# Cross attention over 16 batches on one core: the Gram matrix summed in the same PSUM banks, its turned part made by VectorE

## The chip, the core and the metric

The kernel runs on one core of a Trainium2 chip. The metric is the device time of one execution in microseconds, the median of three runs. In fp32r, TensorE's fast form of fp32, an operand is used with fewer bits than fp32 has; the kernel splits each operand into a hi and a lo part and adds two or three products.

## The reference

Sixteen batches, each with x and a context of 512 channels by 1024 columns. Cut to what is computed:

```python
g_x     = conv1x1(g_w, g_b, ctx).T          # (N, 256)
theta_x = conv1x1(theta_w, theta_b, x).T    # (N, 256)
phi_x   = conv1x1(phi_w, phi_b, ctx)        # (256, N)
W  = theta_x @ phi_x / N                    # (N, N)
y  = (W @ g_x).T                            # (256, N)
wy = conv1x1(w_w, w_b, y)                   # (512, N)
out = bn_gamma * (wy - bn_mean) / sqrt(bn_var + eps) + bn_beta + x
```

Since nothing but products stands between phi and g, the kernel never forms the N x N matrix. It forms the Gram matrix G = ctx ctx^T (512 x 512, symmetric), multiplies the small weights into it, and applies the 256 x 512 result to theta.

## The kernel before, in words

Each batch goes through these steps on TensorE, in this order in one queue.

1. **S and M.** The context lies turned in eight chunks of 128 columns, ctxT_hi and ctxT_lo. With H and L for the two parts, G = H^T H + H^T L + (H^T L)^T, the last product being left out. S = H^T H is formed only in the ten 128x128 blocks of HELD (s_chunk, 32 matmuls), in gbank0 to gbank2. M = H^T L is formed whole, four rows of 128x512, eight matmuls each, in M_BANK, which is wbank4 and wbank0 in turn.
2. **Column sums** of the context (two matmuls).
3. **Turned blocks.** ScalarE has copied M's rows to mt (m_rows); ten matmuls with an identity (`turned`) add the transposed blocks of M to S in the gbanks. VectorE then adds the plain blocks of M from mt and puts the ten finished blocks in stage (`gram_sum`, L534).
4. **First half of theta** (m = 0, its k = 0 and 1). Then six transposes by TensorE (L871) read stage and make the blocks of LOWER, the mirrored ones. They wait for gram_f32. Then the second half of theta, k = 2 and 3.
5. **T blocks** (`t_block`, four blocks of twelve matmuls) multiply G by the phi weights. They wait for gram_lo (L542, all three parts) and low_lo (L591), the lo parts of G that VectorE makes. The fourth T block waits for t_taken, VectorE's copy of the first T block out of its bank (L630).
6. The rest of theta, Q, and the output in eight parts, which VectorE adds to x (L689).

Beside this, for the next batch: VectorE turns the context chunks in 32x32 blocks (L504), ScalarE makes ctxT_hi (`next_hi`, at fixed places of its queue), GpSimd makes ctxT_lo and the running sum per chunk, and after them x_lo (L332). All orders are written out by hand, per engine; semaphores alone tie the engines together. The first batch has its own order (with FIRST_M_BANK) and is not touched by the change. L699 and L357 are the lines of the helpers for every matmul and every ScalarE copy.

Of the kernel before, what the change touches and what calls it, by code (L numbers as in the profile page):

```python
# [27 lines left out]
def xattn_kernel(nc, x, ctx_in, theta_w, theta_b, phi_w, phi_b, g_w, g_b, w_w, w_b,  # L28
# [26 lines left out]

    PLAIN = [(0, 3, 0), (3, 6, 5), (6, 9, 10), (9, 10, 15)]
    T_BANK = [0, 1, 2, 0]
    Q_BANK = [1, 2]
# [8 lines left out]
    with ExitStack() as ctx:  # L67
# [3 lines left out]
        def sem(name):  # L71
            return ctx.enter_context(nc.semaphore(name))
# [44 lines left out]
        scale = sb("scale", [P, KC])  # L117


        m_flat = mt[:, :, :].rearrange("p a b -> p (a b)")  # L120
        t_hi = mt[:, 0:2, :].rearrange("p a (b c) -> p (a b) c", b=2)
        t_lo = mt[:, 2:4, :].rearrange("p a (b c) -> p (a b) c", b=2)
# [34 lines left out]

        M_BANK = [wbank[4], wbank[0], wbank[4], wbank[0]]

# [40 lines left out]
        gram_row = sem("gram_row")  # L200
        m_done, m_made = sem("m_done"), sem("m_made")
        gram_f32 = sem("gram_f32")
        gram_hi_made, gram_lo_made = sem("gram_hi_made"), sem("gram_lo_made")
# [6 lines left out]
        out_done = sem("out_done")  # L210

        def f(ap):

            return ap.bitcast(F32)

# [7 lines left out]
        def gram_bank(place):  # L223

            i = min(place // 3, 2)
            at = place * P - BANK_SPAN[i][0]
            return gbank[i][:, at:at + P]

        def first(b):
# [125 lines left out]
        def _(act):  # L355
# [67 lines left out]
            def body(b, half, par, nxt, nxt2):  # L423
# [4 lines left out]

                def m_rows():
                    for i in range(KC):  # L430
                        if i < KC - 1:
                            act.wait_ge(m_done, (KC - 1) * b + (i + 1))
                        else:
                            next_hi(0)
                            act.wait_ge(gram_chunk, CH * b + CH)
                        hi(mt[:, i, :], M_BANK[i][:, :], m_made)

                def gram_hi_parts():
                    for i, (a, z) in enumerate(BANK_SPAN):
                        act.wait_ge(gram_f32, 3 * b + (i + 1))  # L440
                        hi(gram_hi[:, a:z], stage[:, a:z], gram_hi_made)

                if not first(b):
                    m_rows()
                    next_hi(1)
                    gram_hi_parts()
                    next_hi(2)
# [40 lines left out]
        def _(dve):  # L488
# [39 lines left out]
            def gram_sum(b, i):  # L528
# [7 lines left out]
                if i != 2:  # L536
                    ins.then_inc(gram_f32, 1)

            def gram_lo_part(b, i):
# [36 lines left out]
            def body(b, half, par, nxt, nxt2):  # L576
# [120 lines left out]
        def _(pe):  # L697
# [63 lines left out]
            def body(b, half, par, nxt, nxt2):  # L761
# [11 lines left out]
                if first(b):  # L773
                    for c in range(CH):
                        s_chunk(c)
                        if c == RING:
                            turn_vectors()
                        pe.wait_ge(first_lo, c + 1)
                        for i in range(KC):
                            ins = mm(FIRST_M_BANK[i][:, :], hi_of(c, i), ctxT_lo[:, c, :], c == 0, c == CH - 1)  # L780
                            if i == KC - 1:
                                ins.then_inc(gram_chunk, 1)
                            elif c == CH - 1:
                                ins.then_inc(m_done, 1)
                else:
                    pe.wait_ge(work_free, NO * b + (4 - NO))
                    for c in range(CH):
                        s_chunk(c)
                    for i in range(KC):
                        if i < 2:  # L790
                            pe.wait_ge(work_free, NO * b + ((5, 6)[i] - NO))
                        else:
                            pe.wait_ge(m_made, KC * b + (i - 1))
                        for c in range(CH):
                            if i == 0:
                                pe.wait_ge(ctxT_lo_made, CH * b + (c + 1 - CH))
                            ins = mm(M_BANK[i][:, :], hi_of(c, i), ctxT_lo[:, c, :], c == 0, c == CH - 1)
                            if i == KC - 1:
                                ins.then_inc(gram_chunk, 1)
                        if i < KC - 1:  # L800
                            ins.then_inc(m_done, 1)

# [164 lines left out]
```

## Time and profile before

| | us |
|---|---|
| median of three runs | 783.51 (783.49 to 783.71) |
| the profiled execution | 783.43 |
| its span, first to last instruction | 781.6 |
| TensorE busy | 773.8 (99%) |
| VectorE busy | 495.3 (63%) |
| ScalarE busy | 304.3 (39%) |
| GpSimd busy | 526.5 (67%) |

TensorE's matmuls overlap: a 128x512 one stands for 0.39 us in the rows, but the next starts 0.23 us behind it. So the time of a group of matmuls is read from start to start of the groups, not as a sum of durations. The same holds in a smaller way for VectorE.

### The profile page before, as it was taken

Reading aid. Unit: us, or ns where it says so; the run is one execution under the profiler, and the core shown is the slowest. Engines: PE = TensorE matmul, PEld = TensorE weight load, DVE = VectorE, ACT = ScalarE, POOL = GpSimd, SP = SyncE. Lnnn points to the kernel's source line nnn. Section 1 sums busy time; section 2 is a strip of 40 time slices with the busy share of each in tenths; the row PEclk is TensorE's granted clock in tenths of the full one; section 3 lists DMA queues with packets and bytes.
Section 4 is the critical chain, followed back from the end, with each engine's and each line's share of the span. In section 5 each row is a group of like instructions: output and inputs, shape, how many; then the busy total and the mean of one; then the engine's idle time right before and its main releaser. Section 6 shows DMA issues by size and latency. Waiting matters only on the chain.

```text
span 781.6 us, 11639 instructions
## 1 busy us (share of the span) xinstructions
PE 773.8 (99%) x4066; PEld 668.8 (86%) x4066; DVE 495.3 (63%) x891; ACT 304.3 (39%) x514; POOL 526.5 (67%) x358
## 2 busy tenths in 40 slices
PE   7999999999999999999999999999999999999998
PEld 6688888888888888888888888888888888888887
DVE  3874865749657385664848657396574847658255
ACT  5534533414344243543425345143542325334231
POOL 5939995757858477785758857478685767847500
DMA  9815573370835508264280734608365181740202
GB/s 278 202 67 130 194 188 135 79 245 1 215 107 110 212 22 216 84 161 161 54 252 17 188 134 90 232 0 215 107 132 190 33 229 59 173 150 1 108 1 107
DMA packets 55415, 103.17 MB, mean 132 GB/s; under 512 B 2506, under 2 KB 38244, under 8 KB 55396
## 3 DMA queue, kind: packets, MB, share of 16 engines
q1 hardware_dynamic: 53264, 101.86, 44.6%
q10 hardware_dynamic: 2132, 1.05, 0.6%
q8 instruction: 12, 0.20, 0.1%
q14 instruction: 7, 0.06, 0.0%
HBM read 69.35 MB, written 33.55 MB: 132 GB/s over the span
## 4 chain that ended last, share of the span: by engine, by line
PE 98%; DMA 1%; POOL 0%; DVE 0%; ACTq 0%; ACT 0%; issue 0%
PE wbank L699 58%; PE gbank L699 38%; PE wbank L871 1%; PE wbank L745 1%; DMA ctx_sb<-in_ctx_dram 1%; PE wbank L723 0%; PE wbank L751 0%; POOL ctxT_lo L303 0%; PE wbank L735 0%; DVE ctxT L504 0%; ACT ctxT_hi L357 0%; ACTq L368 0%; DVE x_sb L676 0%; ACTq L142 0%; PE wbank L710 0%
## 5 line engine op out<-in xcount | busy, mean ns | idle before, releaser
L303 POOL TENSOR_TENSOR ctxT_lo<-ctxT,ctxT_hi 128x512 fp32r<-128x512 f32 x124 | 168.0, 1356 | 202.9 <-ACT ctxT_hi L357 202.9
L314 POOL TENSOR_TENSOR ctx_sum<-ctx_sum,ctxT 128x512 f32<-128x512 f32 x108 | 157.8, 1461 | 0.2
L332 POOL TENSOR_TENSOR x_lo<-x_sb,x_hi 128x1024 fp32r<-128x1024 f32 x60 | 142.4, 2410 | 0.0
L357 ACT ACTIVATE mt<-wbank 128x512 fp32r<-128x512 f32 x64 | 37.9, 598 | 230.6 <-PE wbank L699 230.6
L689 DVE SCALAR_TENSOR_TENSOR x_sb<-wbank,const,x_sb 128x512 f32<-128x512 f32 x110 | 77.5, 746 | 69.4 <-PE wbank L699 69.3
L699 PE MATMUL wbank<-ctxT_lo,ctxT_hi 128*128 128x512 f32 x512 | 120.2, 390 | 0.5 <-POOL ctxT_lo L303 0.5
L357 ACT ACTIVATE ctxT_hi<-ctxT 128x512 fp32r<-128x512 f32 x124 | 76.6, 629 | 91.3 <-DVE ctxT L504 91.0
L534 DVE TENSOR_TENSOR stage<-gbank,mt 128x384 f32<-128x384 f32 x64 | 28.3, 485 | 131.7 <-PE gbank L699 131.7
L699 PEld LDWEIGHTS wbank<-ctxT_lo,ctxT_hi 128*128 128x128 f32 x512 | 94.6, 188 | 19.0 <-POOL ctxT_lo L303 0.7
L504 DVE STREAM_TRANSPOSE ctxT<-ctx_sb 128x512 f32<-128x512 f32 x124 | 78.8, 683 | 10.4 <-DMA ctx_sb<-in_ctx_dram 10.3
L699 PEld LDWEIGHTS gbank<-ctxT_hi 128*128 128x128 f32 x512 | 78.9, 189 | 4.0 <-issue 2.3
L699 PE MATMUL wbank<-x_hi,wt_hi 128*128 128x512 f32 x256 | 81.9, 401 | 0.0
L699 PE MATMUL gbank<-ctxT_hi 128*128 128x384 f32 (+1 forms) x512 | 79.7, 311 | 1.9 <-ACT ctxT_hi L357 1.9
L699 PE MATMUL gbank<-z_hi,mt 128*128 128x512 f32 x256 | 81.4, 389 | 0.0
L699 PE MATMUL wbank<-x_lo,wt_hi 128*128 128x512 f32 x256 | 79.5, 392 | 0.0
L699 PE MATMUL wbank<-x_hi,wt_lo 128*128 128x512 f32 x256 | 79.1, 390 | 0.0
L699 PE MATMUL wbank<-th_hi,q_hi 128*128 128x512 f32 (+1 forms) x226 | 72.2, 387 | 0.0
L699 PE MATMUL wbank<-th_hi,q_lo 128*128 128x512 f32 (+1 forms) x226 | 72.2, 387 | 0.0
L699 PE MATMUL wbank<-th_lo,q_hi 128*128 128x512 f32 (+1 forms) x226 | 72.2, 387 | 0.0
L625 DVE TENSOR_TENSOR mt<-stage,mt 128x256 fp32r<-128x256 f32 x64 | 65.8, 1045 | 4.0 <-ACT mt L357 3.6
L357 ACT ACTIVATE x_hi<-x_sb 128x1024 fp32r<-128x1024 f32 x64 | 62.6, 1056 | 0.5 <-DMA x_sb<-in_x_dram 0.5
L542 DVE TENSOR_TENSOR gram_lo<-stage,gram_hi 128x384 fp32r<-128x384 f32 (+1 forms) x48 | 59.9, 1300 | 0.0
(113 smaller groups left out, 1334.4 us busy)
## 6 DMA issues: line engine op xcount, KB each, us to landing
x_sb<-in_x_dram SPq DMA_DIRECT2D x16, 2048.0 KB, 7.7
out_dram<-x_sb SPq DMA_DIRECT2D x63, 512.0 KB, 2.8
ctx_sb<-in_ctx_dram SPq DMA_DIRECT2D x60, 512.0 KB, 8.5
ctx_sb<-in_ctx_dram SPq DMA_DIRECT2D x4, 256.0 KB, 6.2
ctx_sb<-in_ctx_dram ACTq DMA_DIRECT2D x4, 256.0 KB, 7.0
x_sb<-in_L_xattn_w_w_dram SPq DMA_DIRECT2D x1, 512.0 KB, 9.0
stage<-in_L_xattn_theta_w_dram SPq DMA_DIRECT2D x1, 512.0 KB, 14.4
phi_nat<-in_L_xattn_phi_w_dram SPq DMA_DIRECT2D x1, 512.0 KB, 13.5
```

Of the source, the lines that this page charges most:

```text
L303: nc.gpsimd.tensor_tensor(ctxT_lo[:, c, :], turned_ctx(b, c), f(ctxT_hi[:, c, :]), ALU.subtract).then_inc(sem_, 1)
L314: nc.gpsimd.tensor_tensor(ctx_sum[:, :], ctx_sum[:, :], src, ALU.add).then_inc(ctxT_used, 1)
L332: nc.gpsimd.tensor_tensor(x_lo[:, k, :], x_sb[par][:, k, :], f(x_hi[:, k, :]), ALU.subtract).then_inc(x_lo_made, 1)
L357: nc.scalar.activation(dst, src, ACT.Copy).then_inc(sem_, 1)
L504: nc.vector.transpose(turned_ctx(b, c).rearrange("p (k q) -> p k q", q=32), ctx_sb[:, :, 32 * c:32 * c + 32]).then_inc(ctxT_made, 1)
L534: ins = nc.vector.tensor_tensor(stage[:, a * P:z * P], gbank[g][:, at:at + (z - a) * P], f(m_flat[:, m * P:(m + z - a) * P]), ALU.add)
L542: nc.vector.tensor_tensor(gram_lo[:, a:z], stage[:, a:z], f(gram_hi[:, a:z]), ALU.subtract).then_inc(gram_lo_made, 1)
L625: nc.vector.tensor_tensor(t_lo[:, m, :], stage[:, r * CI:(r + 1) * CI], f(t_hi[:, m, :]), ALU.subtract).then_inc(t_lo_made, 1)
L689: nc.vector.scalar_tensor_tensor(out=x_sb[par][:, m, cols], in0=OUT_BANK[m][h][:, :], scalar=const[:, m:m + 1], in1=x_sb[par][:, m, cols], ...
L699: return nc.tensor.matmul(dst, lhsT, rhs, start=start, stop=stop, skip_group_check=True)
L745: ins = nc.tensor.matmul(Z_BANK[j][:, :], g_nat[:, k, j * P:(j + 1) * P], wsT[:, k, :], start=k == 0, stop=k == KI - 1)
L871: ins = nc.tensor.transpose(LOW_BANK[g][:, n * P:(n + 1) * P], held(stage, i, j), ident[:, :])
```

## The change

In all batches but the first, M is now formed first and whole, its four rows in four banks at once (GRAM_BANK: gbank1, gbank2, gbank0, wbank4). VectorE turns those blocks of each row that are wanted mirrored, in 32x32 blocks, straight out of PSUM into stage (`turn_row`; transposes of 2x128, 256, 384 and 384 columns). A 32x32-block transpose leaves each 32x32 block at its old place in the grid, so 32 copies follow, each from one group of 32 partitions to another (`move`, for all 16 pairs (a, d)): 16 for the blocks 0 to 6 and 16 for the blocks 7 to 9. They write mt. TensorE then adds row j of S into row j's bank, on top of M, and waits for row_turned before each row, since the turn must read M without S. VectorE adds the turned blocks from mt to M + S (`gram_row_sum`) and goes on to gram_lo as before. The ten identity matmuls, ScalarE's four copies of M, and the wait for them are gone.

The pieces of the diff below are, in this order, constants and banks, ScalarE's queue, VectorE's and TensorE's.

```diff
+    TURN_COLUMNS = [(0, 3), (0, 1), (0, 1, 2), (1, 2, 3)]
+    TURN_FIRST = [0, 2, 4, 7]
+    TURN_GROUPS = [(0, 7), (7, 10)]
+    GRAM_PLACES = [(0, 3), (3, 6), (6, 8), (8, 10)]
+    DVE_MOVES = [(a, d) for a in range(4) for d in range(4)]
...
-        M_BANK = [wbank[4], wbank[0], wbank[4], wbank[0]]
+        GRAM_BANK = [gbank[1], gbank[2], gbank[0], wbank[4]]
...
+        def move(eng_copy, g, a, d):
+            lo, hi_ = TURN_GROUPS[g]
+            return eng_copy(turned_home[32 * d:32 * d + 32, lo:hi_, 32 * a:32 * a + 32],
+                            turned_here[32 * a:32 * a + 32, lo:hi_, 32 * d:32 * d + 32])
...
                 if not first(b):
-                    m_rows()
+                    gram_hi_part(0)
+                    next_hi(0)
+                    gram_hi_part(1)
                     next_hi(1)
-                    gram_hi_parts()
+                    gram_hi_part(2)
                     next_hi(2)
...
+            def turn_rows(b):
+                def turn_row(i):
+                    dve.wait_ge(m_done, KC * b + i)
+                    m = GRAM_BANK[i]
...
+                        ins = nc.vector.transpose(stage[:, n:n + w].rearrange("p (b q) -> p b q", q=32),
+                                                  m[:, k:k + w].rearrange("p (b q) -> p b q", q=32))
+                    ins.then_inc(row_turned, 1)
+
+                def move_group(g):
+                    dve.wait_ge(row_turned, KC * b + ((3, 4)[g] - KC))
+                    for a, d in DVE_MOVES:
+                        move(nc.vector.tensor_copy, g, a, d).then_inc(moved_by_dve, 1)
+
+                for i in range(3):
+                    turn_row(i)
+                move_group(0)
+                turn_row(3)
+                move_group(1)
+
+            def gram_row_sum(b, j):
+                if j == 0:
+                    dve.wait_ge(moved_by_dve, 2 * len(DVE_MOVES) * b)
+                if j < KC - 1:
+                    dve.wait_ge(gram_row, 3 * b + (j + 1))
+                else:
+                    dve.wait_ge(gram_chunk, CH * b + CH)
+                a, z = GRAM_PLACES[j]
+                ins = nc.vector.tensor_tensor(stage[:, a * P:z * P].rearrange("p (n q) -> p n q", q=P),
+                                              GRAM_BANK[j][:, :].rearrange("p (n q) -> p n q", q=P)[:, GRAM_COLUMNS[j], :],
+                                              f(turned_home[:, GRAM_TURNED[j], :]), ALU.add)
+                if j != 2:
+                    ins.then_inc(gram_f32, 1)
...
                     if nxt:
                         next_ctx()
-                    for i in range(len(PLAIN)):
-                        gram_sum(b, i)
+                    turn_rows(b)
+                    for j in range(KC):
+                        gram_row_sum(b, j)
...
-                    pe.wait_ge(work_free, NO * b + (4 - NO))
-                    for c in range(CH):
-                        s_chunk(c)
                     for i in range(KC):
-                        if i < 2:
-                            pe.wait_ge(work_free, NO * b + ((5, 6)[i] - NO))
-                        else:
-                            pe.wait_ge(m_made, KC * b + (i - 1))
+                        if i >= 2:
+                            pe.wait_ge(work_free, NO * b + ((4, 5)[i - 2] - NO))
                         for c in range(CH):
                             if i == 0:
+                                pe.wait_ge(ctxT_hi_made, CH * b + (c + 1))
                                 pe.wait_ge(ctxT_lo_made, CH * b + (c + 1 - CH))
-                            ins = mm(M_BANK[i][:, :], hi_of(c, i), ctxT_lo[:, c, :], c == 0, c == CH - 1)
...
+                            ins = mm(GRAM_BANK[i][:, :], hi_of(c, i), ctxT_lo[:, c, :], c == 0, False)
+                        ins.then_inc(m_done, 1)
+                    for j in range(KC):
+                        pe.wait_ge(row_turned, KC * b + (j + 1 - KC))
+                        for c in range(CH):
+                            ins = mm(blocks(GRAM_BANK[j][:, :], j), hi_of(c, j), blocks(ctxT_hi[:, c, :], j), False,
+                                     c == CH - 1)
+                            if j == KC - 1:
                                 ins.then_inc(gram_chunk, 1)
...
-                pe.wait_ge(m_made, KC * b + 3)
-                turned(TURNED_EARLY)
-                pe.wait_ge(m_made, KC * b + 4)
-                turned(TURNED_LATE)
+                if first(b):
+                    pe.wait_ge(m_made, 3)
+                    turned(TURNED_EARLY)
+                    pe.wait_ge(m_made, 4)
+                    turned(TURNED_LATE)
```

TensorE's queue in the second batch, before. The 32 matmuls of S stand ahead of these rows; here M, the column sums (into wbank3), the turned blocks (ident_r) and the start of theta:

```order
L699 MATMUL wbank4<-ctxT_lo,ctxT_hi 128x512 x8
L699 MATMUL wbank0<-ctxT_lo,ctxT_hi 128x512 x8
L699 MATMUL wbank4<-ctxT_lo,ctxT_hi 128x512 x8
L699 MATMUL wbank0<-ctxT_lo,ctxT_hi 128x512 x8
L699 MATMUL wbank3<-sum_hi,ones_r 128x512
L699 MATMUL wbank3<-sum_lo,ones_r 128x512
L699 MATMUL gbank0<-ident_r,mt 128x128 x3
L699 MATMUL gbank1<-ident_r,mt 128x128 x2
L699 MATMUL gbank2<-ident_r,mt 128x128 x2
L699 MATMUL gbank1<-ident_r,mt 128x128
L699 MATMUL gbank2<-ident_r,mt 128x128 x2
L699 MATMUL wbank1<-x_hi,wt_hi 128x512
```

The same place of TensorE's queue now. M in four banks, then S in the same four, one row of eight matmuls per bank:

```order
L763 MATMUL gbank1<-ctxT_lo,ctxT_hi 128x512 x8
L763 MATMUL gbank2<-ctxT_lo,ctxT_hi 128x512 x8
L763 MATMUL gbank0<-ctxT_lo,ctxT_hi 128x512 x8
L763 MATMUL wbank4<-ctxT_lo,ctxT_hi 128x512 x8
L763 MATMUL gbank1<-ctxT_hi 128x384 x8
L763 MATMUL gbank2<-ctxT_hi 128x384 x8
L763 MATMUL gbank0<-ctxT_hi 128x256 x8
L763 MATMUL wbank4<-ctxT_hi 128x2x128 x8
L763 MATMUL wbank3<-sum_hi,ones_r 128x512
L763 MATMUL wbank3<-sum_lo,ones_r 128x512
L763 MATMUL wbank1<-x_hi,wt_hi 128x512
```

M has moved ahead of S, S goes row by row instead of chunk by chunk, and the ten identity matmuls are gone.

VectorE's queue in the second batch, before, from the context transposes to the low_lo parts:

```order
L504 STREAM_TRANSPOSE ctxT<-ctx_sb 128x512 x4
L534 TENSOR_TENSOR stage<-gbank0,mt 128x384
L534 TENSOR_TENSOR stage<-gbank1,mt 128x384
L534 TENSOR_TENSOR stage<-gbank2,mt 128x384
L534 TENSOR_TENSOR stage<-gbank2,mt 128x128
L542 TENSOR_TENSOR gram_lo<-stage,gram_hi 128x384 x2
L542 TENSOR_TENSOR gram_lo<-stage,gram_hi 128x512
L591 TENSOR_TENSOR low_lo<-wbank4,low_hi 128x384
L591 TENSOR_TENSOR low_lo<-wbank0,low_hi 128x384
```

And now (CAST is the 32-partition copy; L568 and L573 are the turns out of PSUM):

```order
L527 STREAM_TRANSPOSE ctxT<-ctx_sb 128x512 x4
L568 STREAM_TRANSPOSE stage<-gbank1 128x128 x2
L573 STREAM_TRANSPOSE stage<-gbank2 128x256
L573 STREAM_TRANSPOSE stage<-gbank0 128x384
L256 CAST mt<-stage 32x7x32 x16
L573 STREAM_TRANSPOSE stage<-wbank4 128x384
L256 CAST mt<-stage 32x3x32 x16
L596 TENSOR_TENSOR stage<-gbank1,mt 128x384
L596 TENSOR_TENSOR stage<-gbank2,mt 128x384
L596 TENSOR_TENSOR stage<-gbank0,mt 128x256
L596 TENSOR_TENSOR stage<-wbank4,mt 128x256
L605 TENSOR_TENSOR gram_lo<-stage,gram_hi 128x384 x2
```

Between the context transposes and the sums now stand the turns of rows 0 to 2, sixteen copies, the turn of row 3 and sixteen more copies.

On ScalarE the four copies of M (mt) are gone, and the first ctxT_hi of the next batch, which stood ahead of the last of those copies, now stands behind the first gram_hi.

## Rows read from the trace of the kernel before

**Rows 1.** The page: busy time, share and instructions per engine, and the chain.

```profile
PE 773.8 (99%) x4066; PEld 668.8 (86%) x4066; DVE 495.3 (63%) x891; ACT 304.3 (39%) x514; POOL 526.5 (67%) x358
...
PE 98%; DMA 1%; POOL 0%; DVE 0%; ACTq 0%; ACT 0%; issue 0%
```

**Rows 2.** Timeline of TensorE: start us, us, line, operation, count, idle before.

```profile
9.27 0.83 PE L699 MATMUL gbank<-ctxT_hi 128*128 128x384 f32 x4 [1.85 <-ACT ctxT_hi L357]
...
400.04 4.91 PE L699 MATMUL gbank<-ctxT_hi 128*128 128x384 f32 x32
404.78 7.42 PE L699 MATMUL wbank<-ctxT_lo,ctxT_hi 128*128 128x512 f32 x32
412.04 0.39 PE L699 MATMUL wbank<-sum_hi,ones_r 128*128 128x512 f32 x1
...
412.49 1.23 PE L699 MATMUL gbank<-ident_r,mt 128*128 128x128 f32 x10
413.56 0.68 PE L699 MATMUL wbank<-x_hi,wt_hi 128*128 128x512 f32 x2
...
416.38 0.82 PE L871 MATMUL wbank<-ident,stage 128*128 128x128 f32 x6
...
419.78 0.28 PE L699 MATMUL gbank<-wp_hi,gram_hi 128*128 128x256 f32 x1
...
424.10 0.28 PE L699 MATMUL gbank<-wp_hi,gram_hi 128*128 128x256 f32 x1
```

**Rows 3.** Timeline of VectorE in the same batch.

```profile
401.34 2.48 DVE L504 STREAM_TRANSPOSE ctxT<-ctx_sb 128x512 f32<-128x512 f32 x4
412.97 1.78 DVE L534 TENSOR_TENSOR stage<-gbank,mt 128x384 f32<-128x384 f32 x4 [9.15 <-PE gbank L699]
414.67 3.81 DVE L542 TENSOR_TENSOR gram_lo<-stage,gram_hi 128x384 fp32r<-128x384 f32 x3
418.40 1.01 DVE L591 TENSOR_TENSOR low_lo<-wbank,low_hi 128x384 fp32r<-128x384 f32 x2
...
420.48 1.41 DVE L600 SCALAR_TENSOR_TENSOR th_lo<-wbank,vec_cols,th_hi 128x512 fp32r<-128x512 f32 x2 [0.23 <-ACT th_hi L456]
...
423.02 0.83 DVE L630 SCALAR_TENSOR_TENSOR stage<-bp_row,s_col,gbank 128x256 f32<-128x256 f32 x2
```

**Rows 4.** Timelines of ScalarE (two rows) and GpSimd (two rows).

```profile
410.92 0.62 ACT L357 ACTIVATE ctxT_hi<-ctxT 128x512 fp32r<-128x512 f32 x1
...
413.56 1.85 ACT L357 ACTIVATE gram_hi<-stage 128x384 fp32r<-128x384 f32 x3 [0.21 <-DVE stage L534]
...
392.36 9.49 POOL L332 TENSOR_TENSOR x_lo<-x_sb,x_hi 128x1024 fp32r<-128x1024 f32 x4
411.62 1.28 POOL L303 TENSOR_TENSOR ctxT_lo<-ctxT,ctxT_hi 128x512 fp32r<-128x512 f32 x1 [9.77 <-ACT ctxT_hi L357]
```

**Rows 5.** VectorE's groups, shapes kept apart: shapes, count, busy us, mean ns.

```profile
L504 DVE STREAM_TRANSPOSE ctxT<-ctx_sb 128x512 f32<-128x512 f32 x124 | 78.8, 683 | 10.4 <-DMA ctx_sb<-in_ctx_dram 10.3
...
L534 DVE TENSOR_TENSOR stage<-gbank,mt 128x384 f32<-128x384 f32 x48 | 25.2, 554 | 131.7 <-PE gbank L699 131.7
...
L591 DVE TENSOR_TENSOR low_lo<-wbank,low_hi 128x384 fp32r<-128x384 f32 x32 | 16.2, 544 | 1.1 <-ACT low_hi L357 1.1
...
L534 DVE TENSOR_TENSOR stage<-gbank,mt 128x128 f32<-128x128 f32 x16 | 4.5, 280 | 0.0
...
L572 DVE COPY zb_row<-wbank 128x512 f32<-128x512 f32 x1 | 0.7, 692 | 0.4 <-PE wbank L751 0.4
...
L526 DVE COPY vec_cols<-wbank 128x18 f32<-128x18 f32 x1 | 0.2, 178 | 1.8 <-PE wbank L710 1.8
```

**Rows 6.** Timeline of VectorE: sums of the first batch, gram_lo of the last.

```profile
27.24 1.67 DVE L534 TENSOR_TENSOR stage<-gbank,mt 128x384 f32<-128x384 f32 x4
...
745.67 1.62 DVE L542 TENSOR_TENSOR gram_lo<-stage,gram_hi 128x384 fp32r<-128x384 f32 x3
```

More of the change, by code:

```diff
@@ L117, in xattn_kernel, with f @@
         scale = sb("scale", [P, KC])
+        def f(ap):
+            return ap.bitcast(F32)
         m_flat = mt[:, :, :].rearrange("p a b -> p (a b)")
+        turned_here = stage[:, :].rearrange("p (n q) -> p n q", q=P)
+        turned_home = m_flat[:, 0:UPPER].rearrange("p (n q) -> p n q", q=P)
         t_hi = mt[:, 0:2, :].rearrange("p a (b c) -> p (a b) c", b=2)
@@ L201, in xattn_kernel @@
         m_done, m_made = sem("m_done"), sem("m_made")
+        row_turned = sem("row_turned")
+        moved_by_dve = sem("moved_by_dve")
         gram_f32 = sem("gram_f32")
@@ L210, in xattn_kernel @@
         out_done = sem("out_done")
-        def f(ap):
-            return ap.bitcast(F32)
         def held(tile, j, i):
@@ L227, in gram_bank, with blocks @@
             return gbank[i][:, at:at + P]
+        def blocks(ap, j):
+            if j < KC - 1:
+                return ap[:, GRAM_COLUMNS[j].start * P:GRAM_COLUMNS[j].stop * P]
+            return ap.rearrange("p (k q) -> p k q", q=P)[:, GRAM_COLUMNS[j], :]
+        def move(eng_copy, g, a, d):
+            lo, hi_ = TURN_GROUPS[g]
+            return eng_copy(turned_home[32 * d:32 * d + 32, lo:hi_, 32 * a:32 * a + 32],
+                            turned_here[32 * a:32 * a + 32, lo:hi_, 32 * d:32 * d + 32])
         def first(b):
@@ L427, in next_hi, with gram_hi_part @@
                         ctx_hi(b + 1, c)
[L429 to L432, printed above, removed]
-                        else:
[L434 to L441, printed above, removed]
+                def gram_hi_part(i):
+                    a, z = BANK_SPAN[i]
+                    act.wait_ge(gram_f32, 3 * b + (i + 1))
+                    hi(gram_hi[:, a:z], stage[:, a:z], gram_hi_made)
                 if not first(b):
-                    m_rows()
+                    gram_hi_part(0)
+                    next_hi(0)
+                    gram_hi_part(1)
                     next_hi(1)
-                    gram_hi_parts()
+                    gram_hi_part(2)
                     next_hi(2)
@@ L537, in gram_sum @@
                     ins.then_inc(gram_f32, 1)
+            def turn_rows(b):
+                def turn_row(i):
+                    dve.wait_ge(m_done, KC * b + i)
+                    m = GRAM_BANK[i]
+                    if i == 0:
+                        for n, k in enumerate(TURN_COLUMNS[i]):
+                            ins = nc.vector.transpose(turned_here[:, n, :].rearrange("p (b q) -> p b q", q=32),
+                                                      m[:, k * P:(k + 1) * P].rearrange("p (b q) -> p b q", q=32))
+                    else:
+                        n, k = TURN_FIRST[i] * P, TURN_COLUMNS[i][0] * P
+                        w = len(TURN_COLUMNS[i]) * P
+                        ins = nc.vector.transpose(stage[:, n:n + w].rearrange("p (b q) -> p b q", q=32),
[13 more added lines that the diff above has]
+                    dve.wait_ge(moved_by_dve, 2 * len(DVE_MOVES) * b)
+                if j < KC - 1:
+                    dve.wait_ge(gram_row, 3 * b + (j + 1))
+                else:
+                    dve.wait_ge(gram_chunk, CH * b + CH)
[5 more added lines that the diff above has]
+                    ins.then_inc(gram_f32, 1)
             def gram_lo_part(b, i):
```

8 lines of the change are left out of this document (4 added, 4 removed).

## The prediction

> **What bounds the kernel now.** I read the busy shares and the chain that ended last first [rows 1]: TensorE is busy 99% of the span and holds 98% of the chain, so time is won or lost only where TensorE gets fewer microseconds of work or has to wait. Next the timeline of TensorE in one batch in the middle of the run [rows 2], where the rows follow each other without idle time. I count from the start of S at 400.04 and call that t = 0: S lasts 4.74 us (to 404.78), M 7.26 (to 412.04), the column sums 0.45, the ten turning matmuls 1.07 (412.49 to 413.56), the first half of theta 2.82, the six LOWER transposes with the second half 3.40 (416.38 to 419.78). The first T block starts at t = 19.74, the fourth at 24.06. Then VectorE over the same batch [rows 3]: between its context transposes, which end at 401.34 + 2.48 = 403.82 (t = 3.78), and its first Gram sum it is idle for 9.15 us. Behind that comes a chain without a gap: sums 1.70, gram_lo 3.73, low_lo. The T block needs all of gram_lo and the first low_lo (418.40 + 0.54 [rows 5] = 418.94) and starts at 419.78. So there is only 0.84 us of slack where the new VectorE work ends.
>
> **What goes.** Ten matmuls in each of 15 batches (the first keeps them): 15 x 1.07 = 16.1 us of TensorE time. ScalarE loses four copies of M, which cost nothing (TensorE waited for none). S and M change places, 12.0 us together as before. M now needs all of ctxT_lo 4.74 us earlier. GpSimd makes it ahead of x_lo, whose four instructions start at 392.36 [rows 4], so ctxT_lo is there over 7 us before t = 0. The banks: the latest output copy that M waits for is one of those that end by 401.34 (t = 1.3), and it is wanted for M's fourth row at t = 5.4. None of these costs anything.
>
> **What VectorE gets.** Per batch five 32x32-block transposes out of PSUM (1280 columns) and 32 copies of 32 partitions, 16 of 7x32 = 224 elements and 16 of 3x32 = 96, all in VectorE's one queue, ahead of the sums. The trace has no such copy. From the two COPY rows [rows 5]: 178 ns for 18 elements, 692 for 512, so 1.04 ns an element and 159 ns fixed. Successive instructions overlap a little: three sums of 554 ns and one of 280 add to 1.94 us, and take 1.67 [rows 6], 0.09 us saved for each follower. Upper end: one element a cycle, no overlap: 0.392 and 0.259 us, 16 x 0.651 = 10.4 us a batch. Lower end: overlap as in the row and, since nothing here excludes it for a copy within SBUF, two elements a cycle: 0.186 and 0.119, 4.9 us. One element a cycle with overlap gives 7.5. I take 0.26 us a copy, 8.3 us a batch (4.7 and 3.6 for the two groups): above the middle of the ends (7.65), because the overlap is seen only between instructions that work on the same 128 partitions, while nearly every copy here writes another 32 than the one ahead of it.
>
> Two rules of the Trainium skill bear on this price, both on the page "VectorE: DVE Perf Modes". Its section "Two Vector instructions with no wait between them" says that an instruction whose input or output starts in another group of 32 partitions than the last one is held until all earlier ones have finished; no row here shows it, as all of before's work starts at partition 0. The section "Mode 2×_2P — use both read ports for one tensor" says that a 4-byte copy within SBUF can run at two elements a cycle; the COPY rows read PSUM and show one. By both rules the 32 copies would cost about 7.8 us and the kernel about 798; by the first alone 10.4 us and 837, by the second alone 4.9 us and 767.
>
> **The sum, per batch.** The third M row ends at t = 3 x 7.26/4 + 0.16 = 5.6; rows 0 and 1 are turned before that (from 3.78, two of 0.28 and one of about 0.4). The turn of row 2 is 384 wide: 0.55 us by a fit to 683 ns for 512 [rows 5], to t = 6.2. Sixteen copies to 10.9. Only then is row 3 turned, since it stands behind them in the queue: to 11.5. TensorE wants it earlier: rows 0 to 2 of S end at 7.26 + 4.74 x 1024/1280 = 11.05. **First stall 0.45 us.** Row 3 of S ends at 12.45, column sums and half theta at 15.7. VectorE: the other 16 copies to 15.1, the four sums, which wait for the last copy, 1.75 to 16.9 (with a short wake-up). The LOWER transposes read the sums: **second stall 1.2 us.** They and the second half of theta end at 20.3. gram_lo 3.73 to 20.6, low_lo 0.54 to 21.15; T block at 21.2: **third stall 0.9 us.** Against the 19.74 of before that is +1.46 a batch, which is 2.55 us of stalls less 1.07. Fifteen times that is 22 us. The profiled execution took 783.43 us (span 781.6), against a median of 783.51, no difference. 783.4 + 22 = **805 us**.
>
> Is something later late too? The fourth T block needs the first T copy of VectorE: that ends at 423.02 + 0.46 = 423.48, 4.54 us behind the first low_lo, of which 0.23 is an idle wait for th_hi [rows 3] that goes when VectorE is late; 21.15 + 4.3 = 25.45, and TensorE gets there at 21.2 + 4.32 = 25.5. Just in time. ScalarE's next context chunk now stands behind gram_hi part 0 in its queue: first sum at about 15.7, gram_hi 0.53, ctxT_hi 0.6 [rows 4], so at 16.85 instead of 11.5. GpSimd behind it starts 5.3 us later against 9.77 us of idle time: hidden. The DMA loads hang on transposes that move by no more than 1.5 us.
>
> The price at which it turns: the sums end at 8.6 + (copies), and before's T block start allows 19.74 - 0.05 - 0.54 - 3.73 = 15.4. So 6.8 us a batch, 0.21 us a copy, is no change; at 5.75 us (0.18 a copy) all is hidden and the full 16 us is won; each 0.03 us more a copy costs 15 x 32 x 0.03 = 14 us.
>
> **Rivals.**
> (a) Cheap copies, the other side: VectorE's idle 9.15 us takes everything in. At 4.9 us the sums end at 13.5, low_lo at 17.8, and TensorE arrives at 18.67: 783.4 - 16.05 = 767 us. For it: the idle time is there and the elements are few. Against it: the fixed 0.159 us must then shrink to 0.07 by overlap in all 32. It decides below 0.21 us a copy.
> (b) Dear copies, 0.325 us each, 10.4 us: the turn of row 3 ends at 13.05 (stall 2.0), the sums at 19.0, T block at 23.3: +3.55 x 15 = 53, 837 us. For it: all rows show one element a cycle and this is that rate with every change of partitions paid in full.
> (c) gram_lo gets quick. It takes 3.81 us beside GpSimd's work but 1.62 in the last batch, where GpSimd has none [rows 6]. Since GpSimd now starts later, it could miss gram_lo: then low_lo ends at 19.05, only two stalls are left, T block at 20.3, +0.56 x 15: 792 us. Against it: ctxT_hi is ready at 16.85 and gram_lo starts at 16.9, so they still meet.
> A fall of TensorE's clock in the new gaps I leave out: behind the 1.85 us gap before 9.27 [rows 2] four matmuls took 0.83 us at a granted clock of 1.00, and each gap forecast is shorter.
>
> **Numbers.** Forecast (copies of 7.2 to 9.6 us in all) 0.60, own range 789 to 824; (a) 0.15, of which 0.02 lies at no change; (b) 0.15; (c) 0.10. For what a measurement can tell, 0.2% or 1.6 us counts as a change. Faster 0.13, same 0.03, slower 0.84. The range 780 to 838 leaves out most of (a) and the dearest end of (b).
>
> **What would show it.** In the new profile: 150 turning matmuls gone. The copies as two groups of 240; a mean start-to-start of about 0.29 and 0.23 us. TensorE idle on VectorE at three places of each batch: before row 3 of S, before the LOWER transposes, before the T blocks. VectorE's 9.15 us gap nearly gone. M without a wait for ctxT_lo. GpSimd's gap shorter by some 4 us. I am wrong if TensorE stays without idle time (copies below 0.18 us), if it waits for GpSimd's ctxT_lo or if another place than these three has the longest wait.

## The result

The changed kernel takes 815.37 us (median, 815.24 to 815.52) against 783.61 for the kernel before, measured beside it: ratio 1.0405, 95% interval 1.0388 to 1.0421. It is slower by 31.8 us. Forecast were 805, with a range of 780 to 838. The direction was right, and so was the mechanism in the steady batches, the third to the sixteenth. Of the 31.8 us the forecast had 22; the rest lies in the second batch, which it had not treated apart.

The page of the changed kernel (busy us and share per engine; the granted clock of TensorE in 40 slices; the chain that ended last, by engine and by line), which answers to [rows 1]:

```profile
span 813.4 us, 11915 instructions
...
PE 770.8 (95%) x3916; PEld 654.3 (80%) x3916; DVE 650.9 (80%) x1446; ACT 263.3 (32%) x454; POOL 526.7 (65%) x358
...
PEclk9999799999999999999999999999999999999999
...
PE 74%; DVE 20%; issue 3%; DMA 2%; DVEq 0%; POOL 0%; SPq 0%; ACTq 0%; ACT 0%
PE wbank L763 36%; PE gbank L763 35%; DVE mt L256 14%; DVE stage L596 2%; DVE stage L573 2%; DMA ctx_sb<-in_ctx_dram 2%; PE wbank L938 2%; PE wbank L809 1%; DVE ctxT L527 1%; DVE x_sb L753 0%; PE wbank L787 0%; PE wbank L815 0%; POOL ctxT_lo L333 0%; SPq L280 0%; DVEq L592 0%
```

TensorE has 150 matmuls fewer and is busy 95% of the span instead of 99%. A fifth of the chain (the work that ended last, followed back) now runs over VectorE, 14% of the chain over the 32-partition copies alone (L256). And the clock falls in slice 5, about 81 to 102 us; the page of before has no row of the clock at all.

TensorE in one batch in the middle of the run, as in [rows 2]. M starts at 419.39, which is t = 0:

```profile
419.39 5.60 PE L763 MATMUL gbank<-ctxT_lo,ctxT_hi 128*128 128x512 f32 x24
424.83 1.98 PE L763 MATMUL wbank<-ctxT_lo,ctxT_hi 128*128 128x512 f32 x8
426.64 3.90 PE L763 MATMUL gbank<-ctxT_hi 128*128 128x384 f32 x24
431.33 1.21 PE L763 MATMUL wbank<-ctxT_hi 128*128 128x256 f32 x8 [0.78 <-DVE stage L573]
...
437.12 0.88 PE L938 MATMUL wbank<-ident,stage 128*128 128x128 f32 x6 [1.37 <-DVE stage L596]
...
440.63 0.39 PE L763 MATMUL gbank<-wp_hi,gram_hi 128*128 128x256 f32 x1
```

The same batch on VectorE, which answers to [rows 3]:

```profile
423.09 0.47 DVE L568 STREAM_TRANSPOSE stage<-gbank 128x128 f32<-128x128 f32 x2
423.49 0.41 DVE L573 STREAM_TRANSPOSE stage<-gbank 128x256 f32<-128x256 f32 x1
425.03 0.58 DVE L573 STREAM_TRANSPOSE stage<-gbank 128x384 f32<-128x384 f32 x1 [1.13 <-PE gbank L763]
425.65 5.01 DVE L256 CAST mt<-stage 32x224 fp32r<-32x224 f32 x16
430.69 0.58 DVE L573 STREAM_TRANSPOSE stage<-wbank 128x384 f32<-128x384 f32 x1
431.31 3.93 DVE L256 CAST mt<-stage 32x96 fp32r<-32x96 f32 x16
435.38 1.35 DVE L596 TENSOR_TENSOR stage<-gbank,mt 128x384 f32<-128x384 f32 x3
436.65 0.41 DVE L596 TENSOR_TENSOR stage<-wbank,mt 128x256 f32<-128x256 f32 x1
436.98 3.13 DVE L605 TENSOR_TENSOR gram_lo<-stage,gram_hi 128x384 fp32r<-128x384 f32 x3
440.03 1.01 DVE L655 TENSOR_TENSOR low_lo<-wbank,low_hi 128x384 fp32r<-128x384 f32 x2
```

Two of the three forecast stalls stand in brackets: 0.78 us ahead of S row 3 (forecast 0.45) and 1.37 ahead of the LOWER transposes (1.2). The T block starts at 440.63, t = 21.24; forecast was 21.2, and 19.74 was before. The third stall is the rest: 440.63 - 437.12 = 3.51 us from LOWER to the T block, against 3.40 before, 0.1 us and not 0.9.

**Where the time is.** From one LOWER group to the next, 15 intervals in both kernels. In the kernel before all were 47.28 to 47.29 us but the first, 47.74. Now fourteen are 48.79 to 48.89, and the first is 95.04 - 37.45 = 57.59. So the fourteen cost 22.1 us together (1.58 each), and the second batch alone, which lies in the first interval, costs 9.85. They add to 31.9, the measured 31.8 within 0.1 us. The second batch on TensorE and on VectorE, and TensorE's granted clock (each stretch: busy us with counts, per engine, then clock, DMA share, GB/s):

```profile
74.63 1.98 PE L763 MATMUL wbank<-ctxT_lo,ctxT_hi 128*128 128x512 f32 x8
80.93 6.56 PE L763 MATMUL gbank<-ctxT_hi 128*128 128x384 f32 x24 [4.32 <-DVE stage L568]
89.20 1.47 PE L763 MATMUL wbank<-ctxT_hi 128*128 128x256 f32 x8 [1.71 <-DVE stage L573]
...
95.04 0.82 PE L938 MATMUL wbank<-ident,stage 128*128 128x128 f32 x6
```

```profile
77.99 2.49 DVE L527 STREAM_TRANSPOSE ctxT<-ctx_sb 128x512 f32<-128x512 f32 x4 [7.76 <-DMA ctx_sb<-in_ctx_dram]
...
81.70 6.83 DVE L256 CAST mt<-stage 32x224 fp32r<-32x224 f32 x16
```

```profile
80.00:82.00 2.00, 1.07 (x3) 1.07 (x4) 1.97 (x6) 0.00 (x0) 2.00 (x2) 0.50 0.99 404
82.00:84.00 2.00, 2.00 (x8) 2.00 (x8) 1.97 (x2) 0.00 (x0) 1.66 (x1) 0.50 0.06 23
...
90.00:92.00 2.00, 2.00 (x8) 1.71 (x7) 1.75 (x9) 0.00 (x0) 0.00 (x0) 0.50 0.45 184
```

VectorE waits until 77.99 for the context of the third batch. The turns are queued behind that, so TensorE waits 4.32 us before row 0 of S. Then the clock is 0.50 (1.2 GHz), and 24 matmuls of S take from 80.93 to about 87.5, 6.56 us instead of 3.90. The 16 copies take 6.83 us where they take 5.01 later, and row 3 waits another 1.71 us. Soon behind that wait the clock is 0.50 a second time, and from row 3 to LOWER it takes 5.84 us instead of the 4.2 that the forecast has for the same matmuls (0.95 + 0.45 + 2.82).

### The profile page after: what moved, and what is told of

It is laid out like the page before. It is cut to its first block, busy times and chain, and to the rows that moved or that the text cites. A ratio compares the mean times of both kernels' runs of the same rounds, so it can differ in the third digit from the quotient of the medians.

```text
span 813.4 us, 11915 instructions
## 1 busy us (share of the span) xinstructions
PE 770.8 (95%) x3916; PEld 654.3 (80%) x3916; DVE 650.9 (80%) x1446; ACT 263.3 (32%) x454; POOL 526.7 (65%) x358
## 4 chain that ended last, share of the span: by engine, by line
PE 74%; DVE 20%; issue 3%; DMA 2%; DVEq 0%; POOL 0%; SPq 0%; ACTq 0%; ACT 0%
PE wbank L763 36%; PE gbank L763 35%; DVE mt L256 14%; DVE stage L596 2%; DVE stage L573 2%; DMA ctx_sb<-in_ctx_dram 2%; PE wbank L938 2%; PE wbank L809 1%; DVE ctxT L527 1%; DVE x_sb L753 0%; PE wbank L787 0%; PE wbank L815 0%; POOL ctxT_lo L333 0%; SPq L280 0%; DVEq L592 0%
## 5 line engine op out<-in xcount | busy, mean ns | idle before, releaser
L333 POOL TENSOR_TENSOR ctxT_lo<-ctxT,ctxT_hi 128x512 fp32r<-128x512 f32 x124 | 175.8, 1419 | 234.7 <-ACT ctxT_hi L387 234.7
L344 POOL TENSOR_TENSOR ctx_sum<-ctx_sum,ctxT 128x512 f32<-128x512 f32 x108 | 146.8, 1359 | 0.2
L387 ACT ACTIVATE gram_hi<-stage 128x384 fp32r<-128x384 f32 (+1 forms) x48 | 26.3, 550 | 338.0 <-DVE stage L596 337.1
L256 DVE CAST mt<-stage 32x224 fp32r<-32x224 f32 (+1 forms) x480 | 122.0, 254 | 15.0
L763 PE MATMUL gbank<-ctxT_lo,ctxT_hi 128*128 128x512 f32 x360 | 84.3, 389 | 0.1
L763 PEld LDWEIGHTS gbank<-ctxT_lo,ctxT_hi 128*128 128x128 f32 x360 | 67.5, 188 | 14.4 <-issue 0.5
L689 DVE TENSOR_TENSOR mt<-stage,mt 128x256 fp32r<-128x256 f32 x64 | 70.8, 1123 | 3.9 <-ACT mt L387 3.6
L763 PEld LDWEIGHTS gbank<-ctxT_hi 128*128 128x128 f32 x392 | 66.4, 194 | 7.2 <-DVE stage L568 4.7
L763 PE MATMUL gbank<-ctxT_hi 128*128 128x384 f32 (+1 forms) x392 | 67.3, 325 | 4.7 <-DVE stage L568 4.3
L664 DVE SCALAR_TENSOR_TENSOR th_lo<-wbank,vec_cols,th_hi 128x512 fp32r<-128x512 f32 x64 | 45.0, 743 | 17.6 <-ACT th_hi L479 17.6
```

Source lines behind the costliest of these rows:

```text
L256: return eng_copy(turned_home[32 * d:32 * d + 32, lo:hi_, 32 * a:32 * a + 32], turned_here[32 * a:32 * a + 32, lo:hi_, 32 * d:32 * d + 32])
L333: nc.gpsimd.tensor_tensor(ctxT_lo[:, c, :], turned_ctx(b, c), f(ctxT_hi[:, c, :]), ALU.subtract).then_inc(sem_, 1)
L344: nc.gpsimd.tensor_tensor(ctx_sum[:, :], ctx_sum[:, :], src, ALU.add).then_inc(ctxT_used, 1)
L387: nc.scalar.activation(dst, src, ACT.Copy).then_inc(sem_, 1)
L664: nc.vector.scalar_tensor_tensor(out=th_lo[:, m, cols], in0=TH_BANK[m][h][:, :], scalar=bt_col[:, m:m + 1], in1=f(th_hi[:, m, cols]), op0= ...
L689: nc.vector.tensor_tensor(t_lo[:, m, :], stage[:, r * CI:(r + 1) * CI], f(t_hi[:, m, :]), ALU.subtract).then_inc(t_lo_made, 1)
```

## The experiments

The theory after the result: (1) VectorE's chain turns, copies, sums, gram_lo, low_lo sets the steady batch, with a threshold below which it is hidden; (2) a 32-partition copy cannot overlap the one ahead when it changes the group of partitions; (3) the second batch's 9.85 us come from the DMA wait ahead of the turns. The rivals stand in the expectations. "Interval" is the time from one LOWER group to the next.

### The chain, not the stalls

```diff
-                for i in range(3):
+                for i in range(4):
                     turn_row(i)
                 move_group(0)
-                turn_row(3)
                 move_group(1)
```

> All four rows of M are turned before the first of the 32 copies, in all batches. My theory: the end of VectorE's chain sets the batch, not the sum of TensorE's stalls; the copies must wait for M's fourth row, 1.1 to 1.2 us later, so each batch gets about 1.1 us longer although TensorE's first stall (0.78 us, ahead of S row 3) disappears: period 50.0 us, 831 us. Rival: each stall of TensorE counts for itself; then 15 x 0.78 us is won, 804 us.

848.75 us, ratio 1.0841 (1.0822 to 1.0859). The stall ahead of S row 3 is gone, and the batch is longer, as the theory said and against the rival. But the interval is 51.2 us, not 50.0. TensorE in one batch:

```profile
444.25 1.12 PE L762 MATMUL wbank<-ctxT_hi 128*128 128x256 f32 x8
...
452.02 1.54 PE L937 MATMUL wbank<-ident,stage 128*128 128x128 f32 x6 [3.44 <-DVE stage L595]
453.21 1.20 PE L762 MATMUL wbank<-x_hi,wt_hi 128*128 128x512 f32 x2
...
455.07 0.64 PE L762 MATMUL wbank<-x_hi,wt_lo 128*128 128x512 f32 x2
```

```profile
452.00:455.00 3.00, 2.98 (x10) 2.66 (x11) 3.00 (x4) 3.00 (x7) 3.00 (x3) 0.50 0.00 0
```

What had been two short stalls is one of 3.44 us, and behind it the clock is 0.50 for about 3 us: the six transposes take 1.19 us from their start to that of the next group (0.57 in the kernel before, 416.38 to 416.95), and the following matmuls are slow too. From LOWER to the T blocks it takes 4.91 us instead of 3.51, which covers the additional 1.2 us. The size was missed, by a cost that the expectation did not contain.

### No copies at all

```diff
-    DVE_MOVES = [(a, d) for a in range(4) for d in range(4)]
+    DVE_MOVES = []
```

(and the wait for them is left out). The turned part of G is then not put in its place.

> All 32 copies left out (the turned part of the Gram matrix is then not brought to its place). My theory: all that remains is hidden, TensorE has no stall in the steady batches and their period falls to 47.28 - 1.07 = 46.2 us; the second batch keeps its wait for the context DMA and its low clock, about 8 us over before's 47.7. Sum 783.4 + 8 - 15 = 776 us. Rival (the turns out of PSUM or the order M then S cost something by themselves): the steady period stays above 46.5 us, 781 us or more.

773.18 us, ratio 0.9872 (0.9855 to 0.9888). The interval is 46.11 us, 1.17 less than before: everything else that the change adds is hidden, and a little more than the ten matmuls' 1.07 us is won (the other 0.1 us is not explained). The first interval is 53.09, 5.35 over before (I had expected 8).

### Three copies in four

```diff
-    DVE_MOVES = [(a, d) for a in range(4) for d in range(4)]
+    DVE_MOVES = [(a, d) for a in range(4) for d in range(4) if a != d]
```

> 24 of the 32 copies (those that stay in their own group of 32 partitions are left out, so part of the turned blocks is missing). At the measured 0.28 us a copy that is 6.75 us of copies a batch, just at the break-even that the prediction worked out (6.8). My theory, with gram_lo at 3.1 us as in the new profile: stalls of at most 0.3 us a batch are left, period 46.5 us, and with the second batch's 8 us 781 us. By the prediction's own terms (gram_lo 3.73) the period would be 47.2 and the time 791. Rival (every copy costs in proportion, no threshold: 1.59 + 1.07 = 2.66 us a batch over 32 copies): period 48.2 us, 806 us.

781.91 us, ratio 0.9985 (0.9975 to 0.9994), interval 46.63. So 24 copies cost 0.52 us a batch over none, and the last eight cost 48.87 - 46.63 = 2.24, 0.28 each, which is the full time from one copy to the next. That is a threshold, and no cost in proportion. The whole time is near that of the kernel before because two things cancel: the steady batches win 14 x 0.65 = 9.1 us, and the first interval, 55.18, is 7.4 above before's. VectorE's rows for the 24:

```profile
410.00 3.75 DVE L256 CAST mt<-stage 32x224 fp32r<-32x224 f32 x12
...
414.39 2.95 DVE L256 CAST mt<-stage 32x96 fp32r<-32x96 f32 x12
```

### What one copy costs

Both versions cut each copy of 7 blocks in 4 and 3; they differ only in the order of the 32 pieces.

```diff
-    TURN_GROUPS = [(0, 7), (7, 10)]
+    TURN_GROUPS = [(0, 4), (7, 10), (4, 7)]
...
                     for a, d in DVE_MOVES:
-                        move(nc.vector.tensor_copy, g, a, d).then_inc(moved_by_dve, 1)
+                        for part in ((0, 2), (1,))[g]:
+                            move(nc.vector.tensor_copy, part, a, d).then_inc(moved_by_dve, 1)
```

That is with the pieces of a pair together (the sums wait for 48 copies a batch in both versions). Apart:

```diff
-                    for a, d in DVE_MOVES:
-                        move(nc.vector.tensor_copy, g, a, d).then_inc(moved_by_dve, 1)
+                    for part in ((0, 2), (1,))[g]:
+                        for a, d in DVE_MOVES:
+                            move(nc.vector.tensor_copy, part, a, d).then_inc(moved_by_dve, 1)
```

> Each copy of 7 blocks is cut in two (4 and 3 blocks), both between the same two groups of 32 partitions, one right behind the other. 16 more copies a batch. My theory: a copy that reads or writes another group of partitions than the one ahead of it cannot overlap it (start to start 0.025 us above its duration in the new profile), one that keeps both groups can (about 0.09 us below). Durations 0.226 and 0.217 us: a pair costs 0.24 + 0.14 = 0.38 us against 0.315 for the uncut copy, +1.0 us a batch: 831 us. Rival (no hold; the fixed cost is paid by every copy alike): the same time as the other cut version, about 858 us.

> The same cut copies, but all 16 of 4 blocks first and then all 16 of 3 blocks, so that every one changes a group of partitions. My theory: 0.25 + 0.245 us for what was 0.315, +2.9 us a batch: 858 us, 1.9 us a batch more than with the pairs kept together. Rival: no difference between the two orders.

833.25 us (ratio 1.0629, 1.0611 to 1.0647) and 863.66 (1.1022, 1.1004 to 1.1040). The 32 pieces on VectorE, together and apart:

```profile
385.28 6.12 DVE L256 CAST mt<-stage 32x128 fp32r<-32x128 f32 x32
```

```profile
395.83 7.93 DVE L256 CAST mt<-stage 32x128 fp32r<-32x128 f32 x32
```

The same work takes 6.12 us or 7.93. A pair together is 0.38 us, as expected; apart it is 0.50. The row's shape is that of its first instruction; durations (means of 227 and 213 to 217 ns) hardly differ. So it is the overlap that goes when a copy changes its group of partitions. Theory (2) holds, with 0.11 us for each copy that could have overlapped. (The totals also contain TensorE's low clock in some batches, so the price is read from VectorE's rows.)

### The copies shared with ScalarE

```diff
-    DVE_MOVES = [(a, d) for a in range(4) for d in range(4)]
+    MOVES = [(a, d) for a in range(4) for d in range(4)]
+    DVE_MOVES, ACT_MOVES = MOVES[0:9], MOVES[9:16]
...
                 if not first(b):
+                    for g in range(2):
+                        act.wait_ge(row_turned, KC * b + ((3, 4)[g] - KC))
+                        for a, d in ACT_MOVES:
+                            move(lambda o, i: nc.scalar.activation(o, i, ACT.Copy), g, a, d).then_inc(moved_by_act, 1)
                     gram_hi_part(0)
```

> Seven of the 16 copies of each group are made by ScalarE, which is idle for 22 us at that time; VectorE keeps nine. My theory: VectorE then ends 14 copies (3.9 us) earlier, the sums end at about t = 13.6 and TensorE has no stall in the steady batches: period 46.2 us. The second batch keeps its DMA wait and low clock (+8): 776 us. Rival (the copies of the two engines hinder each other, or ScalarE's take over 0.55 us each): period 47 us or more, 787 us or more.

The sums wait for both engines' copies. 773.18 us, ratio 0.9867 (0.9851 to 0.9884): faster than both kernels. The interval is 46.11, that of no copies at all. ScalarE's seven of each group take as long as VectorE's nine:

```profile
405.18 2.80 DVE L257 CAST mt<-stage 32x224 fp32r<-32x224 f32 x9
...
408.50 2.19 DVE L257 CAST mt<-stage 32x96 fp32r<-32x96 f32 x9
```

```profile
405.18 2.86 ACT L469 ACTIVATE mt<-stage 32x224 fp32r<-32x224 f32 x7 [12.11 <-DVE stage L578]
408.50 2.10 ACT L469 ACTIVATE mt<-stage 32x96 fp32r<-32x96 f32 x7 [0.46 <-DVE stage L578]
```

### The second batch

In the second batch alone the context chunks are turned later:

```diff
-                    if nxt:
+                    ctx_late = isinstance(b, int) and b == 1
+                    if nxt and not ctx_late:
                         next_ctx()
                     turn_rows(b)
+                    if nxt and ctx_late:
+                        next_ctx()
```

> In the second batch alone, VectorE turns the next context's chunks behind the turns and copies instead of ahead of them. My theory: of the 31.8 us that the change costs, 9.85 stand in the second batch, where VectorE waits for the context DMA with the turns of M queued behind that wait; TensorE then waits 4.3 us and runs S at half clock. With the DMA wait out of the way the LOWER transposes of that batch come at about 91 instead of 95.04 us and S runs at 2.4 GHz: 809 to 812 us. Rival: the second batch is slow because GpSimd's x_lo slows the copies (6.83 us against 5.01 in later batches); then no more than 1 us is won, 814 to 815.

817.19 us, ratio 1.0436 (1.0419 to 1.0454). It won nothing, and my theory (3) fell in this form; the rival named GpSimd and the copies, though not that they cost as much. VectorE and GpSimd in that batch:

```profile
75.74 12.22 DVE L256 CAST mt<-stage 32x224 fp32r<-32x224 f32 x16
87.99 0.58 DVE L573 STREAM_TRANSPOSE stage<-wbank 128x384 f32<-128x384 f32 x1
```

```profile
74.61 9.42 POOL L362 TENSOR_TENSOR x_lo<-x_sb,x_hi 128x1024 fp32r<-128x1024 f32 x4
```

Sixteen copies take 12.22 us. The first four start at 75.74, 77.18, 79.55 and 81.89. From the second on they are 2.35 us apart, which is the length of one x_lo (9.42 for four); GpSimd is done at 84.0, and from 84.21 the other twelve run in 3.75 us, 0.31 each. S row 3 waited 7.99 us. So in the changed kernel the DMA wait had kept most of the copies away from x_lo, and without it they ran into it.

With the shared copies the same change:

> The shared copies together with the late context chunks of the second batch. My theory: both costs are gone, 783.4 - 15 x 1.07 = 767.4, and up to 3 us more for the context chunks in the second batch: 767 to 771 us. Rival for the second batch (its cost is not the DMA wait): no faster than the shared version alone.

774.59 us, ratio 0.9883 (0.9867 to 0.9900), 1.4 us more than the shared version: a miss, for the same reason (VectorE's nine copies take 10.05 us there). Next, ScalarE makes all 32 copies in the second batch, with the chunks late and with the chunks ahead:

```diff
-                    for a, d in DVE_MOVES:
+                    for a, d in () if isinstance(b, int) and b == 1 else DVE_MOVES:
...
-                        for a, d in ACT_MOVES:
+                        for a, d in (MOVES if isinstance(b, int) and b == 1 else ACT_MOVES):
```

> As the shared version with the late context chunks, but in the second batch ScalarE makes all 32 copies and VectorE none. My theory of the second batch: VectorE's copies and GpSimd's x_lo instructions take turns (one copy per GpSimd instruction of 2.3 us), which is why the late context chunks won nothing; ScalarE's copies are free of that. ScalarE's first 16 (0.41 us each) then run from 75.8 to 82.3, the other 16 (0.30) to 87.1, the LOWER transposes come at about 89.5 instead of 91.3 with the shared version: 771 us. Rival (GpSimd slows whoever touches SBUF): ScalarE's copies stretch too, LOWER at 95 or later, 777 us or more.

> The same, with the context chunks of the second batch ahead of the turns again, as in the changed kernel. This leaves the wait for the context DMA (to 78 us) as the only difference from the run with the late chunks. My theory: the turns start at 80.5, the first copies at 82, the last at 93.2, the LOWER transposes at about 95: 5 to 6 us later than with the late chunks, 777 us. Rival (the DMA wait is hidden): within 1 us of the other.

772.43 us (0.9857, 0.9840 to 0.9873) and 779.35 (0.9956, 0.9939 to 0.9973). ScalarE beside the same x_lo of GpSimd, chunks late:

```profile
75.70 11.47 ACT L469 ACTIVATE mt<-stage 32x224 fp32r<-32x224 f32 x32 [4.93 <-DVE stage L578]
```

The 32 copies take 11.47 us, where I had reckoned with 11.3, and 11.46 in the other run, where most of them come behind x_lo. So GpSimd does not slow ScalarE. LOWER comes at 88.94 with the late chunks and at 95.11 behind the DMA wait: 6.2 us, against the rival. The times differ by 3.8 us in the profiled runs. The two have these stalls ahead of LOWER, the late chunks first; then the clock of the second behind its stall:

```profile
88.94 1.54 PE L948 MATMUL wbank<-ident,stage 128*128 128x128 f32 x6 [4.17 <-DVE stage L603]
```

```profile
95.11 0.87 PE L945 MATMUL wbank<-ident,stage 128*128 128x128 f32 x6 [3.31 <-DVE stage L603]
```

```profile
95.00:100.00 5.00, 4.89 (x29) 4.10 (x30) 5.00 (x15) 4.51 (x10) 4.86 (x4) 1.00 0.01 2
```

Behind 4.17 us the clock is 0.50 (88 to 94), and the next interval is 48.89 us. Behind 3.31 us it stays at 1.00, and the next interval is 46.38. That takes back 2.5 of the 6.2 us. The single times of the second run spread from 777 to 782 us, which I leave unexplained.

Last, GpSimd kept busy while VectorE copies, in every batch, by eight instructions whose result is not used:

```diff
                     prep_x(b + 1, 1 - par)
+                    pool.wait_ge(sum_split, 2 * b + 4)
+                    for k in range(8):
+                        if k:
+                            pool.wait_ge(busied, 8 * b + k)
+                        nc.gpsimd.tensor_tensor(ctx_sum[:, :], phi_nat[:, 0, :], phi_nat[:, 1, :], ALU.subtract).then_inc(busied, 1)
```

> The changed kernel with eight more GpSimd tensor_tensor of 128x512 (1.3 us each, results unused) in every batch behind x_lo, so that GpSimd is busy until about t = 14 while VectorE copies. My theory: VectorE's copies get through only between GpSimd's instructions, about one per 1.3 us; six copies take 7.8 us instead of 1.9, group one ends about 5.9 us later, 14 batches: +83 us, and TensorE's longer stalls bring it to half clock for a while as in the runs with stalls above 3 us: 900 to 930 us. Rival (bandwidth is shared evenly): copies twice as long during that time, +2.5 us a batch, about 850 us. Rival (no contention): 815.

912.96 us, ratio 1.1648 (1.1629 to 1.1668), inside the range that only taking turns gave. VectorE's and GpSimd's rows of one batch:

```profile
416.97 11.15 DVE L257 CAST mt<-stage 32x224 fp32r<-32x224 f32 x16
428.15 0.58 DVE L581 STREAM_TRANSPOSE stage<-wbank 128x384 f32<-128x384 f32 x1
```

```profile
414.24 10.89 POOL L387 TENSOR_TENSOR ctx_sum<-phi_nat 128x512 f32<-128x512 f32 x8
```

GpSimd works until 425.1. VectorE's 16 copies take 11.15 us instead of 5.01, 6.1 us more (expected 5.9).

## Why the prediction was right, and where it was short

**TensorE's 16.1 us less.** Right: without copies 1.17 us a batch is won, against 1.07 forecast. M ahead of S, the banks and ctxT_lo cost nothing, as forecast; GpSimd's ctxT_lo was never waited for in the steady batches. Its gap ahead of the first chunk grew from 9.8 to 14.1 us, where I had said it would shrink by 4: the later start was partly made up in the gaps behind it. That sign to look for was wrong, the claim that the shift is hidden was right.

**The price of a copy.** Forecast 0.26 us, 8.3 a batch. Measured 5.01 and 3.93 us, with 0.6 us between them, 8.9 together, 0.28 a copy. Mean durations are 291 and 217 ns (none in the batch shown is over 289; the second batch has one that GpSimd holds up):

```profile
L256 DVE CAST mt<-stage 32x224 fp32r<-32x224 f32 x240 | 69.9, 291 | 7.6
L256 DVE CAST mt<-stage 32x96 fp32r<-32x96 f32 x240 | 52.1, 217 | 7.5
```

Less the fixed 159 ns of [rows 5] they leave 132 ns for 224 elements, 0.59 ns each, near half of the 1.04 ns of the COPY rows that read PSUM. That is what the Trainium skill, page "VectorE: DVE Perf Modes", section "Mode 2×_2P — use both read ports for one tensor", says of 4-byte copies within SBUF, two elements a cycle, and the trace agrees. Start to start they take 0.315 us (5.01 - 0.29 over 15), 0.02 to 0.03 more than they last, and the two cut versions show that the overlap of [rows 6] is lost with the change of partitions. That agrees with the Trainium skill, the same page, section "Two Vector instructions with no wait between them". Both rules at once describe what the copies do, though their 7.8 us is farther from the measured 8.9 than my 8.3. That my value came nearer was luck: it lay between two ends, one with the slow rate and one with the overlap, and the trace shows neither.

**The sum of a batch.** Forecast +1.46 us, measured 1.58. The chain ended the sums at t = 17.6 (forecast 16.9) by the dearer copies; gram_lo then took 3.05 us from start to start of low_lo instead of 3.73. So two terms were off by 0.7 us with opposite signs, and that the T block came at t = 21.24 with 21.2 forecast is luck to that extent. Case (c), a quick gram_lo, was partly true. GpSimd did meet gram_lo, at 437.09 with gram_lo at 436.98, as the forecast had it, and the first two parts took what they took before (0.55 and 1.64 us, against 0.55 and 1.65). Only the third was shorter, 1.10 instead of 1.77; GpSimd ran a plain copy (ctx_sum, 0.94 us) in that time and tensor_tensors before, but no run shows that this is the reason. The break-even was forecast at 6.8 us, too low by the shorter gram_lo: with 24 copies of 6.7 us the interval is 46.63, still 0.65 below before's 47.28. The ratio of 0.9985 looks like break-even only because the second batch took back what the steady ones won.

**The step that failed** is "Is something later late too?", which asked this only of a batch in the middle. In the second batch VectorE waits for the context DMA. The wait was visible in [rows 5]: the row of the context transposes ends in 10.3 us idle, released by DMA. Of this, 7.90 us stand in the second batch of the kernel before:

```profile
78.31 2.49 DVE L504 STREAM_TRANSPOSE ctxT<-ctx_sb 128x512 f32<-128x512 f32 x4 [7.90 <-DMA ctx_sb<-in_ctx_dram]
81.97 1.78 DVE L534 TENSOR_TENSOR stage<-gbank,mt 128x384 f32<-128x384 f32 x4 [1.16 <-PE gbank L699]
```

There the sums still had to wait for TensorE, so nothing on TensorE's path hung on the DMA wait. The change put the turns behind it in VectorE's queue, and TensorE waits for these. I had listed what stands in that queue between the transposes and the sums, and had not asked what the transposes themselves wait for. It cost 9.85 us: two stalls of 4.32 and 1.71 us, 2.7 us of low clock in 24 matmuls of S and some 1.6 behind row 3, less 1.07 for the matmuls gone. The last 0.6 us is overlap between matmuls that the stalls undo: S starts 12.09 us behind M instead of 7.25, 4.84 more for an idle time of 4.32. How the 9.85 split between the DMA wait and GpSimd is not settled by one number, since taking one away brings in the other. What the runs show is that either alone is dear: without copies, with the DMA wait left, the interval was 5.35 us above before's 47.74; with the late chunks, and GpSimd against the copies, 11.2 above it. With neither, when ScalarE makes the copies and the chunks are late, it was 51.19, still 3.45 above, with ScalarE's longer copies and the low clock in it.

**The clock.** I had left it out because each gap forecast was shorter than 1.85 us. In the steady batches that was right (granted clock 1.00 from 126 to 175 us). The gap of the second batch was not among them.

## What to carry to other kernels

Work added to an engine with idle time is free only up to the slack of the wait that ends last. Work out that threshold in us per instruction before the change: here 24 copies cost 0.52 us a batch together, and the next eight 2.24. When work is put in a queue, look at what stands ahead of it there in the first and last rounds too, DMA waits above all. Small copies can be shared with an engine that is idle at that time: here ScalarE took seven of sixteen, TensorE's interval was the same as with no copies at all, and 815 us became 773.

## What was not expected of the hardware

VectorE's copies within SBUF and GpSimd's tensor_tensor take turns: a copy of 0.29 us lasts up to 2.34 us beside an x_lo of 2.4, and 16 copies 11 to 12 us instead of 5.0. ScalarE's copies of the same blocks are not touched. VectorE's gram_lo, a tensor_tensor with two inputs in SBUF, is slowed beside GpSimd too, to 3.8 us from 1.6 [rows 3, 6].

The Trainium skill, page "SBUF — State Buffer", section "SBUF: two separate sides", has this as a lock: VectorE in a two-port mode, or with two SBUF inputs against a GpSimd instruction that reads SBUF, shares one pair of ports with GpSimd; the one that starts first holds it for its whole instruction, and ScalarE never waits for it. The trace agrees: a copy starts and waits for one whole x_lo, 2.35 us from one to the next, and ScalarE's 32 copies take 11.47 us beside GpSimd. Had I weighed that rule before, it would have changed nothing in the steady batch, where GpSimd is idle from t = 3.6 to the end of the copies, and would have pointed to the second one: in the kernel before, x_lo runs there from 74.51 for 9.49 us, where the copies of the first three rows would start.

TensorE's granted clock was 0.50 behind stalls of 3.44, 4.17, 4.32 and 7.99 us and 1.00 behind those of 0.78 and 1.37. The length of the stall alone does not settle it: behind the 3.31 us of the run with ScalarE's copies it stayed at 1.00, and in the changed kernel's second batch it was 0.50 again from 90 to 92 us, behind a stall of 1.71 us that followed the one of 4.32. Where the clock falls, the stall is paid twice: by 1.2 us more a batch with all four rows turned first, and by 2.7 in the 24 matmuls of S behind the stall of 4.32.
